# A cross-attention and FP4-style feed-forward layer on one core: every engine's order up to tile 5 rewritten, more PSUM banks for the value products, the last tile's h turned by four DMAs

## The reference

```python
# cross-attention
q = layernorm(x) @ Wq.T + bq;  k = ctx @ Wk.T;  v = ctx @ Wv.T + bv
x = x + tanh(g_xattn) * (softmax(q @ k.T / sqrt(512)) @ v @ Wo.T + bo)
# feed-forward; Q(a): blocks of 16, scale = max|a|/6, values rounded to 0, .5, 1, 1.5, 2, 3, 4, 6 times the scale
h = silu(Q(layernorm(x)) @ Q(w_gate).T) * (Q(layernorm(x)) @ Q(w_up).T)     # 1408 columns
x = x + tanh(g_ffn) * (Q(h) @ Q(w_down).T)
```

## Time and profile before

| | |
|---|---|
| Median of 3 runs | 873.81 us (872.18 to 874.11) |
| Profiled execution | 871.96 us |
| Its span | 870.1 us (1.86 us less than its time) |
| PE busy | 854.3 us, 98% of the span |
| DVE, ACT, POOL busy | 677.6, 375.4, 369.6 us |
| Mean granted TensorE clock | 0.998 of 2.4 GHz |

### The profile page before, as it was taken

One profiled execution on the slowest core, in us unless ns is written; L12 is line 12 of the kernel. 1 busy time (PEld: TensorE's weight loads), 2 busy tenths in 40 slices (PEclk: granted clock), 3 DMA queues, 4 the chain that ended last, 5 costly groups with the idle time before them and its releaser, 6 DMA issues.

```text
span 870.1 us, 11646 instructions
## 1 busy us (share of the span) xinstructions
PE 854.3 (98%) x4252; PEld 444.6 (51%) x4252; DVE 677.6 (78%) x1056; ACT 375.4 (43%) x661; POOL 369.6 (42%) x364
## 2 busy tenths in 40 slices
PE   9899998999999999999999999999999999999997
PEld 5565545544554455444544455445544554444443
DVE  5899989689878777878688867886787778777753
ACT  3565575732453354434353345334533544333320
POOL 4497466234433353334343434344333533333321
PEclk9999999999999999999999999999999999999999
DMA  9723020144225332632052224422232323333222
GB/s 318 259 71 112 15 62 13 33 105 108 58 57 121 57 58 58 120 62 62 21 122 58 58 59 100 87 57 58 59 74 53 58 59 75 58 58 64 58 46 69
DMA packets 149311, 67.45 MB, mean 78 GB/s; under 512 B 133011, under 2 KB 134405, under 8 KB 149255
## 3 DMA queue, kind: packets, MB, share of 16 engines
q1 hardware_dynamic: 149255, 66.72, 33.4%
HBM read 22.76 MB, written 8.39 MB: 36 GB/s over the span
## 4 chain that ended last, share of the span: by engine, by line
PE 69%; issue 2%; DVE 1%; DMA 1%; POOL 0%; ACT 0%; POOLq 0%; ACTq 0%; SPq 0%
PE banks L1453 44%; PE banks L1561 22%; PE banks L1447 1%; PE banks L1528 1%; DMA arena<-h_parts 1%; PE banks L1527 1%; DVE arena L1050 0%; POOL arena L518 0%; DVE arena L1048 0%; DVE h_parts L1207 0%; DVE ring L1212 0%; ACT arena L660 0%; ACT h_parts L793 0%; ACT xnT L747 0%; POOLq L47 0%
## 5 line engine op out<-in xcount | busy, mean ns | idle before, releaser
L1453 PE MATMUL banks<-wgu_hi,x_T 128*128 128x512 f16 (+1 forms) x1536 | 440.4, 361 | 1.9 <-DVE ring L1259 1.0
L1453 PE MATMUL banks<-wgu_lo,x_T 128*128 128x512 f16 (+1 forms) x768 | 277.5, 361 | 0.0
L1561 PE MATMUL banks<-wd,arena 128*128 128x512 f16 x1056 | 234.8, 379 | 1.5 <-DMA arena<-h_parts 1.5
L1453 PEld LDWEIGHTS banks<-wgu_hi,x_T 128*128 128x128 f16 x1536 | 150.2, 98 | 156.5 <-DVE arena L1188 1.3
L1561 PEld LDWEIGHTS banks<-wd,arena 128*128 128x128 f16 x1056 | 103.3, 98 | 121.2 <-DVE ring L1212 2.0
L518 POOL TENSOR_TENSOR arena<-arena,h_r 128x1024 f32<-128x1024 f32 (+1 forms) x60 | 103.4, 1723 | 122.0 <-DVE h_r L1002 122.0
L518 POOL TENSOR_TENSOR arena<-arena,h_s 128x1024 f32<-128x1024 f32 x64 | 88.8, 1389 | 126.5 <-issue 85.0
L781 ACT ACTIVATE arena<-banks,scal 128x512 f32<-128x512 f32 (+1 forms) x96 | 62.0, 646 | 146.8 <-PE banks L1453 146.7
L1453 PEld LDWEIGHTS banks<-wgu_lo,x_T 128*128 128x128 f16 x768 | 75.1, 98 | 77.5 <-issue 1.3
L518 POOL TENSOR_TENSOR xwork<-xwork,x_s 128x512 f32<-128x512 f32 x32 | 34.1, 1066 | 173.2 <-DVE xwork L1050 173.2
L1188 DVE SCALAR_TENSOR_TENSOR arena<-arena,scal,banks 128x512 f32<-128x512 f32 (+1 forms) x90 | 60.8, 676 | 36.4 <-PE banks L1453 28.4
(11 more groups left out here) (156 smaller groups left out, 950.0 us busy)
## 6 DMA issues: line engine op xcount, KB each, us to landing
ring<-in_x_dram SPq DMA_DIRECT2D x8, 1024.0 KB, 5.8
out_dram<-ring SPq DMA_DIRECT2D x32, 256.0 KB, 2.0
arena<-in_L_ffn_w_down_dram SPq DMA_DIRECT2D x4, 704.0 KB, 4.0
arena<-in_L_ffn_w_gate_dram SPq DMA_DIRECT2D x5, 512.0 KB, 10.1
arena<-in_L_ffn_w_up_dram SPq DMA_DIRECT2D x5, 512.0 KB, 10.4
ring<-in_L_xattn_Wk_dram SPq DMA_DIRECT2D x4, 256.0 KB, 5.7
ring<-in_L_xattn_Wq_dram SPq DMA_DIRECT2D x4, 256.0 KB, 6.7
wd<-in_ctx_dram SPq DMA_DIRECT2D x1, 1024.0 KB
```

What stands on the lines that cost most here:

```text
L1453: ended = e.matmul(at, l, r, start=(i == 0), stop=(i == len(terms) - 1))
L1561: ended = e.matmul(down_ps(t)[:, :], l, r, start=(k == 0 and i == 0), stop=(k == KH - 1 and i == 2))
```

## The change

It changes no arithmetic. It does five things.

1. The start-up and tiles 0 to 5 are queued in another order on all five engines (the calls are moved; loops and helpers stay).
2. The five value products, which shared banks 0 and 1, get banks 4, 0, 1, 5, 4; the one-row products gu_top and gu_pow move to banks 4 and 5.
3. h of the last tile is turned by four DMAs instead of one: high and low halves of part 0, counted by h_turned, then of part 1, counted by the new semaphore last_turned. Groups 0 and 1 of the last down product wait only for part 0.
4. The maximum over the values of batches 2 to 7 is turned on TensorE one product later, and its spread later still (step "mid"). On VectorE x_stats(5) and x_stats(6) come ahead of work they stood behind.
5. x_turn(5) is issued ahead of h_turn(3).

```diff
-        mm = [("bqk_row", 0)] + [("key", i) for i in range(KEYS_HALF)] + [("vo", m) for m in range(KD)] + [("bvwo", 0), ("val", 0)]
-        mm += [("key", i) for i in range(KEYS_HALF, 2 * KEYS_HALF)] + [("val", r) for r in range(1, CT)]
+        mm = [("bqk_row", 0)] + [("key", i) for i in range(KEYS_HALF)] + [("vo", m) for m in range(KD)] + [("bvwo", 0)]
+        mm += [("key", i) for i in range(KEYS_HALF, 2 * KEYS_HALF)]
         mm_bank = {name: n % 2 for n, name in enumerate(mm)}
+        mm_bank |= {("val", r): (4, 0, 1, 5, 4)[r] for r in range(CT)}
...
             def h_turn(t):
+                if t >= 2:
+                    w.wait_ge(down_mm, t - 1)
+                if t == NT - 1:
+                    for i, turned in ((0, h_turned), (1, last_turned)):
+                        w.wait_ge(h_lo[i], t + 1)
+                        for p in range(2):
+                            cols = slice(p * HID + PARTS[i].start, p * HID + PARTS[i].stop)
+                            e.dma_start_transpose(h_T[t % 2][:, cols.start // P:cols.stop // P, :], h_parts[:, cols]).then_inc(turned, 16)
+                    return
...
@@ ScalarE @@
             key_copy(3)
+            wo_copy(0)
+            wo_copy(1)
+            key_copy(4)
+            wo_copy(2)
             gu_folds(0, EARLY)
-            key_copy(4)
+            wo_copy(3)
...
                 if j == 4:
                     key_copy(5)
-                    prob_copy(0)
-                if j == 5:
+                if j == 6:
                     x_apply(0)
...
             gate_silu(0, 0)
-            x_squares(2)
             ln1_apply(1)
+            x_apply(2)
+            down_high(0)
+            gate_silu(0, 1)
+            x_squares(2)
+            down_low(0)
...
@@ VectorE @@
-            for j in range(5, NPAIR):
+            for j in range(5, 8):
                 gu_round(j)
             value_row()
             softmax(0)
-            down_tops(0)
+            gu_round(8)
+            sums(0)
             value_rows(0)
...
@@ TensorE @@
+            key_product(0)
             take(turn_bank["bqk", 0], (bqk_sb, 1))
...
+            wo_turn(0)
+            wo_turn(1)
+            power_spread("gu_pow", pow_gu, gu_pow, gu_pow_mm, p_ready)
             key_product(4)
-            power_spread("gu_pow", pow_gu, gu_pow, gu_pow_mm, p_ready)
+            wo_turn(2)
+            wo_turn(3)
...
             gate_up(0, 1, 1)
+            down_turn(0)
             gate_up(0, 2, 0)
+            down_subtract(0)
             gate_up(0, 2, 1)
-            attention_part(0, "a3")
-            attention_part(0, "a4")
-            down_turn(0)
+            att_turn(1, 0)
+            att_turn(1, 1)
             gate_up(1, 0, 0)
-            down_subtract(0)
+            att_scores(1, 0)
+            att_scores(1, 1)
+            att_turn(1, 2)
+            att_turn(1, 3)
             gate_up(1, 0, 1)
...
-                w.wait_ge(h_turned, 16 * (t + 1))
+                w.wait_ge(h_turned, 16 * (t + 1 if t < NT - 1 else NT + 1))
+                if t == NT - 1 and part_of(g):
+                    w.wait_ge(last_turned, 32)
```

More of the change, by code:

```diff
@@ L265, in rows_of @@
             return min(P, ROWS - r * P)
-        first = [("bias", 0)] + [("ctx", r) for r in range(CT)] + [("bqk", 0), ("gu_top", 0), ("gu_pow", 0)]
-        first += [("wo", r) for r in range(KD)]
+        first = [("bias", 0)] + [("ctx", r) for r in range(CT)] + [("bqk", 0)] + [("wo", r) for r in range(KD)]
         turns = [("d_top", 0), ("d_pow", 0)]
@@ L602, in pool_program @@
                 gu_times(j)
-            for j in range(6, NPAIR):
+            for j in range(6, 10):
                 gu_times(j)
@@ L611, in pool_program @@
             x_times(1)
+            down_times(0)
+            x_stats(2)
             down_divide(2)
+            down_times(1)
+            x_times(2)
             down_divide(3)
[L614 to L617, removed]
             x_stats(3)
@@ L637, in pool_program @@
             h_divide(3, 1)
+            x_stats(5)
             h_times(3, 0)
+            x_times(5)
+            h_times(3, 1)
             for t in range(4, NT):
-                h_times(t - 1, 1)
-                if t + 1 < NT:
+                if t == 5:
+                    x_stats(t + 1)
+                if t > 4:
+                    h_times(t - 1, 1)
+                if 5 < t < NT - 1:
                     x_stats(t + 1)
@@ L835, in scalar_program @@
                 e.copy(w_T[:, m, :], bank[QK_BANKS[m]][:, 0:D]).then_inc(qk_sb, 1)
-            w.wait_ge(bias_turned, 1)
-            e.copy(bias_cols[:, :], bank[turn_bank["bias", 0]][:, 0:2 * KD]).then_inc(bias_sb, 1)
+                if m == 2:
+                    w.wait_ge(bias_turned, 1)
+                    e.copy(bias_cols[:, :], bank[turn_bank["bias", 0]][:, 0:2 * KD]).then_inc(bias_sb, 1)
             for r in range(CT):
@@ L880, in scalar_program @@
                 if j == 5:
+                    prob_copy(0)
                     key_copy(6)
                 if j == 6:
-                    x_squares(0)
+                    key_copy(7)
                 if j == 7:
                     key_copy(8)
+                if j == 8:
                     x_high(0)
                     x_apply(1)
-                if j == 8:
-                    x_squares(1)
-                if j == 9:
+                if j == 10:
                     down_folds()
                     down_squares(0)
-                if j == 10:
-                    x_apply(2)
-                    down_squares(1)
+                    x_high(1)
                 gu_low(2 * j)
@@ L1420, in vector_program @@
                 h_scales(t, 1)
+                if t == 4:
+                    x_stats(t + 2)
                 h_round(t, 0)
@@ L1617, in key_product, with wo_turn @@
                 product(bank[mm_bank["key", i]][:, 0:HALF], terms).then_inc(key_mm, 1)
+            def wo_turn(r):
+                take(turn_bank["wo", r], (wo_sb, r + 1))
+                w.wait_ge(loads["wo"], 16)
+                turn(turn_bank["wo", r], [stage_b[:, r, k * P:(k + 1) * P] for k in range(KD)]).then_inc(wo_turned, 1)
             def vo_product(m):
```

279 lines of the change are left out of this document (155 added, 124 removed).

## The result

| | before | changed |
|---|---|---|
| Median | 872.99 us (871.58 to 874.11, 4 runs) | 863.87 us (863.17 to 864.48, 4 runs) |
| Profiled execution, span | 871.96, 870.1 us | 863.36, 861.6 us |
| PE busy | 854.3 us, 98% | 850.2 us, 99% |
| DVE, ACT, POOL busy | 677.6, 375.4, 369.6 us | 677.5, 375.3, 361.2 us |

The ratio is 0.9896 with a 95% interval of 0.9876 to 0.9916: 9.1 us faster. The forecast was 862.9 us, with a range of 859.5 to 868.5.

What follows compares the result with a forecast made beforehand. TensorE bounds the kernel, busy without a gap from 240.2 to 829.5 us. Gains of 2.0 + 9.7 - 2.2 + 1.4 = 10.9 us take 871.96 to 861.1, as a median 862.9 us; range 859.5 to 868.5.

Steps and rivals of the forecast that it cites:

- the forecast's own signs: In the new profile: no TensorE wait above 1 us up to tile 5; steady loop starting at least 9 us earlier.
- Start-up up to the first Wo product: Before TensorE's first Wo product: three waits costing 2.9 us go, about 0.9 us of new wait; gain 2.0 us.
- What a gap costs: TensorE before 240 us: 6.6 us idle, 1.4 for nine gaps' extra cost, 1.7 for the clock; 9.7 us together.
- the dip costs 1.7 us: TensorE's clock at 0.57 from 88 to 92 us, after waiting for gu_high, was priced at 1.7 us.
- New waits: Under the new orders, 2.2 us of new TensorE waits, an estimate, bounds 0 and 9.7.
- five places with next to no slack: down_turn(0), down_subtract(0), att_turn(1, 0), down_subtract(1), att_values(1, 0): waits of 0.3 us at three, 0.65 at two.
- The gap near 239 should go: TensorE's gap near 239 us goes because x_stats(6) no longer stands behind the maximum over the values; no separate size.
- hidden(3, 0): TensorE's wait of 0.91 us for this VectorE result should go, as 6.5 us of VectorE's work moved behind it.
- The end: Last down product, with four DMAs, starts near 858.15 instead of 859.54: 1.4 us gained; bounds 1.5 gained, 0.3 lost.
- rival 2: Last tile's four DMAs gain nothing because each transpose starts only when the previous has landed: 864.6 us; chance 0.08.
- Rival 1: VectorE becomes the bound in early tiles, its idling at value_row delaying its queue: 866.7 or 870.8 us; chance 0.20.
- Rival 3: Slower: VectorE's queue is also held up by GpSimd, TensorE 15 to 17 us late, 878 to 880 us; chance 0.06.

Runs made afterwards that it cites:

- the kernel with all repairs: Changed kernel with x_apply(3) behind down_high(1), x_stats(6) ahead of h_times(4, 0), last h's high half first, last Wo copy ahead of gu_folds: 858.81 us, ratio 0.9841.
- end-alone kernel: Kernel before with only the last tile's h turned by four DMAs: 870.94 us, ratio 0.9974.
- ScalarE's order alone: Kernel before with x_apply(0) behind gu_high of round 6 and x_squares(0) behind gu_low on ScalarE: 873.21 us, ratio 1.0.
- the two bank experiments: Changed kernel with value products back in banks 0 and 1: 880.02 us; kernel before with only the five banks added: 872.03 us, ratio 0.9987.
- the experiment: Changed kernel with VectorE's value_row and softmax(0) again behind the roundings of pairs 8 and 9: 864.58 us.
- half turns: Kernel before with every h turned by two DMAs of 11 blocks instead of one: 872.10 us.

## Why the prediction was right, and where it was not

The time was right: 862.9 us forecast, 863.87 measured, and a gain of 10.9 forecast, of 9.1 measured (8.6 start to start in the traces). A part of how close it came is luck: the forecast was taken off a median of 873.81, and the kernel before now has 872.99, from which the same gain would give 862.1. Two of the forecast's own signs also went against it: TensorE has two waits above 1 us behind its first Wo product (1.74 and 1.35), and down(3), from which on the two kernels run alike, starts 7.5 us earlier (243.99 against 251.50), not 9 or more. By its steps:

**Start-up up to the first Wo product: 2.0 forecast, 0.70 measured.** This is the term that was mis-sized. The wait behind the last Wo copy, taken at 0.9 between bounds of 0 and 2.1, was 1.26: ScalarE does key_copy(4), a Wo copy, gu_folds and the last Wo copy one after another from 40.43 to 42.38 us. Two waits for loads (0.72 and 0.51) took what was left: behind a faster start-up stands the DMA. Over all profiled executions the first Wo product lies at 42.6 to 43.8 us in five of the old order and at 42.0 to 42.7 in seven with this start-up, and at 41.3 in an eighth (the kernel with all repairs has another start-up); the gain is near 0.9 us and its noise nearly as large.

**What a gap costs, 42 to 110 us: the sum right, the reason wrong.** By the forecast's terms this stretch was to gain 1.35 + 0.16 for the gap, 1.7 for the clock, 1.04 + 0.16 for the fifth value_rows: 4.4 us; it gained 5.06. But "the dip costs 1.7 us ... the largest loss of the trace" does not hold. The end-alone kernel had the gap and no dip and got no farther; with ScalarE's order alone the gap and the dip came elsewhere, at the same distance. A wait was read as a loss where a later wait on another engine absorbed it. VectorE set the time, and the forecast had its share in hand (28.56 of 30.50 us) but took VectorE for a bound that might come, not for the one that was there. What freed TensorE was the pair of the banks and the order, as the two bank experiments show.

**New waits, 2.2 forecast: 2.3 at one place of the five, and 1.5 where none was foreseen.** Of the five places with next to no slack only down_subtract(1) waited, 1.74 us (before, it waited 0.91), with 0.16 for the drained end and 0.44 for its slower matmuls 2.34 in all. The reason is the one named (behind x_apply(3), and so behind GpSimd). An even spread over suspects came near the sum by luck; the place was one where an engine change stood ahead of the copy that TensorE needs.

**The gap near 239 should go: it did not.** It was 0.30 us and became 1.35. The forecast looked at VectorE, where x_stats(6) did come early, and missed that GpSimd's half of it was still queued behind h_times(4, 0). With it, the waits left between 42 and 252 us cost 3.9 us, not 2.2; what was saved elsewhere was more than forecast, so that this stretch gained 6.8 us of the 7.5 forecast (9.7 less 2.2).

**hidden(3, 0)** is not waited for any more, as forecast; VectorE finished it at about 183 us, before TensorE needed it.

**The end: 1.4 forecast, 1.08 measured.** The pieces overlapped, so rival 2 falls. Issuing part 0 began at 846.24, 1.4 us behind the start of h_low (844.81), a little later than the forecast put it, and 0.45 us of wait are left.

**Rival 1** (VectorE's idle time before value_row delays everything behind it): 2.95 us idle instead of the 4.1 foreseen, and worth nothing, by the experiment. TensorE runs into SP's queue near 272 us and into VectorE near 278, and only once it is another 1.6 us earlier. **Rival 3** did not come; the GpSimd collisions it feared are in the rows at 136 to 145 us, and cost one wait on TensorE.

## What to carry to other kernels

A wait in a trace is worth its length only if no later wait on the same path grows when it goes: before pricing one, look whether a wait on an engine that was hardly ever idle follows (here some 100 matmuls later), and take that engine's chain as the clock. Moving an operation on one engine does nothing while its other half (here GpSimd's part of the statistics) stands behind something slow in another queue. Once a large reordering has landed, read its remaining waits back through the queues: four small edits gave another 5.2 us here, of which the traces put 3.8 at the edited places; the whole change had 9.1.

## What the runs showed of the hardware

**The clock can fall behind a gap or not, and what it costs depends on the slack.** The same instructions behind the same wait of 1.35 us ran at 0.57 of the clock for 4 us in the kernel before and in the one with half turns, and at full clock in the end-alone kernel; what decides it is not shown. Before gate_up(0, 0, 0) of the old order the dip cost nothing (73.32 us with it, 73.34 without). Behind the wait at 142 us of the changed order it cost all of its 1.7 us, as the run with value_row behind the roundings shows, since nothing behind it absorbs it. The spans agree, though where their clocks fell was not seen: of eight executions of the changed kernel four had a mean clock of 1.00 and a median span of 861.55 us, four had 0.998 and 862.65; in the kernel before, 21 at 1.00 have a median of 870.8 and 12 at 0.998 one of 870.2 (four at 0.997 have 872.7). The repaired kernel, without that wait, had 1.00 in all five.

**GpSimd's small operations stretch beside VectorE, and VectorE beside GpSimd.** GpSimd's operation on rstd takes 0.57 us at 232.65 and took 1.93 at 138.03, with VectorE's operations of 1.62 us running beside it; VectorE's of 1.62 took 4.03 when it began 0.03 us behind a GpSimd operation of 2.58. 2.58 and 1.62 make 4.20. The Trainium skill, "SBUF — State Buffer", section "SBUF: two separate sides", has the two engines' shared ports as an exclusive lock that the first one keeps for its whole instruction, among others where VectorE's has two inputs in SBUF, as this one has, and GpSimd's reads SBUF; the trace agrees, 4.03 us against 4.20 by the rule. The 1.93 us fit it too: the VectorE operation of 137.91 ended 1.50 us after GpSimd's had begun, and 1.50 and 0.57 make 2.07. So a statistic of a few elements on GpSimd is no cheap step where VectorE streams.

**Issuing a transposing DMA on SP** took about 1.25 us for 3 and for 8 blocks, 1.53 for 11 and 3.33 for 22; pieces issued in a row landed 2.4 to 3.3 us after their own start, so they overlap. The forecast had two pieces of 3 blocks at 1.2 us (856.2 to 857.4) where they took about 2.5; it made no difference, since part 1 was covered by 24 matmuls.
